# First layer's scores of B with C computed by halves of the source positions, two halves of the array at a time

## The reference, cut to what matters

```python
xc, Bc, Cc = silu(conv(x_ssm)), silu(conv(Bm)), silu(conv(Cm))   # 32 heads: 64, 128, 128 channels
decay = exp(dt * A)
dtx = dt[..., None] * xc
def step(h, inp):
    dec_t, dtx_t, B_t, C_t = inp
    h = dec_t[..., None, None] * h + dtx_t[..., None] * B_t[:, :, None, :]
    return h, einsum('bhpn,bhn->bhp', h, C_t)
y = y * rsqrt(mean(y * y, axis=-1) + 1e-06) * silu(z)
out = y.reshape(B, T, H * P) @ Wout.T
```

## Time and profile before

| what | before |
|---|---|
| time, median of 3 runs | 1088.79 us |
| profiled execution | 1084.22 us, span 1083.0 us, granted clock 0.994 |
| TensorE matmul busy | 1028.9 us (95%) |
| VectorE busy | 798.6 us (74%) |
| ScalarE busy | 614.9 us (57%) |
| GpSimd busy | 696.9 us (64%) |
| scores L778 | 512 instructions, 62.5 us |
| masks L1733 | 64 instructions, 42.3 us |
| first layer | up to about 572 us |

### The profile page before, as it was taken

How to read it: one execution, slowest core, us unless ns; L and a number is a source line. 1 busy time by engine, 2 the same in 40 slices (tenths; PEclk the granted TensorE clock), 3 DMA queues, 4 the chain that set the end, 5 groups by cost and what they waited for, 6 DMA issues and landing times.

```text
span 1083.0 us, 23866 instructions
## 1 busy us (share of the span) xinstructions
PE 1028.9 (95%) x9886; PEld 851.0 (79%) x9886; DVE 798.6 (74%) x1194; ACT 614.9 (57%) x951; POOL 696.9 (64%) x684
## 2 busy tenths in 40 slices
PE   7899999999999999999999899998888889899998
PEld 6688888888888888888887788887554578788887
DVE  5789887888878888788957676455758875686554
ACT  5897877777778778787625222224863553332221
POOL 4977786787867878678782587554266323285553
PEclk9999999999999999999999999999999999999999
DMA  3322211212112121111020553303121120253311
GB/s 111 113 69 79 69 60 50 69 51 69 60 50 69 50 70 59 50 40 51 2 70 4 187 188 103 102 20 108 47 53 23 30 72 2 82 171 108 114 54 40
DMA packets 47453, 76.29 MB, mean 70 GB/s; under 512 B 11430, under 2 KB 34322, under 8 KB 47346
## 3 DMA queue, kind: packets, MB, share of 16 engines
q1 hardware_dynamic: 47346, 74.77, 21.9%
HBM read 68.46 MB, written 2.36 MB: 65 GB/s over the span
## 4 chain that ended last, share of the span: by engine, by line
PE 64%; DVE 19%; POOL 7%; ACT 4%; issue 3%; DMA 1%; SPq 0%; DVEq 0%; POOLq 0%; ACTq 0%
PE psum L698 33%; PE psum L936 8%; DVE arena L1708 6%; PE psum L670 4%; PE psum L786 4%; PE psum L778 3%; PE psum L831 3%; DVE arena L1745 2%; PE psum L1045 2%; PE psum L1009 1%; DVE arena L1982 1%; PE psum L1079 1%; DVE arena L1764 1%; DVE arena L1772 1%; PE psum L1018 1%
## 5 line engine op out<-in xcount | busy, mean ns | idle before, releaser
L698 PE MATMUL psum<-vT,split 128*128 128x512 f32 x2136 | 536.4, 400 | 12.9 <-DVE arena L1708 5.4
L698 PEld LDWEIGHTS psum<-vT,split 128*128 128x128 f32 x2136 | 388.4, 188 | 102.9 <-DVE arena L1708 7.6
L1708 DVE SCALAR_TENSOR_TENSOR arena<-psum,arena 128x1023 f32<-128x1023 f32 (+2 forms) x208 | 265.7, 1278 | 75.5 <-ACT arena L1237 52.3
L2168 POOL TENSOR_TENSOR split<-arena,split 128x256 fp32r<-128x256 f32 x178 | 134.7, 770 | 66.2 <-ACT split L1162 66.0
L2375 POOL TENSOR_TENSOR arena<-arena,bcast 128x512 f32<-128x512 f32 x64 | 85.7, 1341 | 98.8 <-ACT arena L1409 81.8
L1237 ACT ACTIVATE arena<-psum,arena 128x512 f32<-128x512 f32 x160 | 109.3, 691 | 69.9 <-PE psum L698 69.1
L1409 ACT ACTIVATE arena<-psum,arena 128x512 f32<-128x512 f32 x72 | 49.7, 690 | 165.5 <-PE psum L698 164.5
L1860 DVE SCALAR_TENSOR_TENSOR arena<-psum,arena 128x512 f32<-128x512 f32 x72 | 53.9, 749 | 102.7 <-POOL arena L2375 101.0
L936 PEld LDWEIGHTS psum<-split_down,split_hid 128*128 128x128 f32 x864 | 112.6, 191 | 9.5 <-DVE split_hid L1873 3.7
L936 PE MATMUL psum<-split_down,split_hid 128*128 128x256 f32 x864 | 115.2, 283 | 3.0 <-DVE split_hid L1873 3.0
L2195 POOL TENSOR_TENSOR arena<-arena,v 128x1021 f32<-128x1021 f32 x32 | 76.5, 2390 | 42.4 <-DVE arena L1708 42.4
(11 more groups left out here) (228 smaller groups left out, 1519.9 us busy)
## 6 DMA issues: line engine op xcount, KB each, us to landing
bcast<-scratch_a SPq DMA_DIRECT2D x32, 512.0 KB, 3.7
bcast<-scratch_e SPq DMA_DIRECT2D x32, 512.0 KB, 4.2
arena<-in_w_a SPq DMA_DIRECT2D x16, 768.0 KB, 4.4
arena<-in_wg SPq DMA_DIRECT2D x36, 128.0 KB, 3.6
arena<-in_wu SPq DMA_DIRECT2D x36, 128.0 KB, 3.6
arena<-in_wd SPq DMA_DIRECT2D x36, 128.0 KB, 3.9
arena<-in_wout_a SPq DMA_DIRECT2D x8, 256.0 KB, 2.6
arena<-in_w_b SPq DMA_DIRECT2D x10, 128.0 KB, 5.2
```

The lines of the kernel that those rows point to most:

```text
L698: m = pe.matmul(bank, split[:, t % SPLITS, i, q, :], vT[:, j, q, half * BANK:(half + 1) * BANK], start=(n == 0), stop=(n == 3 * KD - 1))
L1708: dve.scalar_tensor_tensor(out=tile[:, s:T], in0=bank[:, 0:T - s], scalar=cw_a[:, j, i, TAPS - 1 - s:TAPS - s], in1=tile[:, s:T], op0=ALU. ...
L2168: pool.tensor_tensor(split[:, t % SPLITS, 1], raw, split[:, t % SPLITS, 0].bitcast(F32), ALU.subtract).then_inc(sem["split"], 1)
```

## The change

For every chunk the scores are computed in two matmuls: `late=0` takes the sources 0 to 63 against all 128 targets, `late=1` the sources 64 to 127 against the targets 64 to 127; the masked quarter isn't computed. For even chunks the first goes to the PSUM partitions 0 to 63 and the second to 64 to 127; for odd chunks it is the other way round. Matmuls of an even and an odd chunk alternate: c late 0, c+1 late 0, c late 1, c+1 late 1. A bank of four chunks has 8 matmuls in place of 4, of 64 output rows each. One semaphore, `masked_a`, is added; nothing waits on it.

The mask, one instruction over 128 partitions and 512 elements before, becomes three: the even chunks of the bank (128 partitions, 256 elements), the odd chunks' sources 0 to 63 (64 partitions, 256 elements, scores read from PSUM partitions 64 to 127), and the odd chunks' sources 64 to 127 (64 partitions, 128 elements, scores read from PSUM partitions 0 to 63). The result lies in SBUF where it lay before.

```diff
+        def half_of(c, late):
+            at = (late + c) % 2 * SUB
+            return slice(at, at + SUB)
...
-                    for i in range(4):
-                        c = 4 * q + i
-                        m = pe.matmul(chunk(bank, i), chunk(cv_a[:, j % 2, 1 + g, :], c),
-                                      chunk(cv_a[:, j % 2, 3 + g, :], c), start=True, stop=True)
+                    def rows(c, late):
+                        ts = slice(late * SUB, P)
+                        return pe.matmul(chunk(bank, c % 4)[half_of(c, late), ts],
+                                         chunk(cv_a[:, j % 2, 1 + g, :], c)[:, late * SUB:(late + 1) * SUB],
+                                         chunk(cv_a[:, j % 2, 3 + g, :], c)[:, ts], start=True, stop=True)
+                    for c in (4 * q, 4 * q + 2):
+                        for late in range(2):
+                            rows(c, late)
+                            m = rows(c + 1, late)
                     m.then_inc(sem["unit"], 1)
...
-                    dve.tensor_tensor(half, bank_of(unit), half, ALU.mult).then_inc(sem["dve_done"], 1)
+                    buf, scores = (ap.rearrange("p (c o t) -> p c o t", o=2, t=P) for ap in (half, bank_of(unit)))
+                    dve.tensor_tensor(buf[:, :, 0], scores[:, :, 0], buf[:, :, 0], ALU.mult).then_inc(sem["masked_a"], 1)
+                    for late in range(2):
+                        own, ts = slice(late * SUB, (late + 1) * SUB), slice(late * SUB, P)
+                        m = dve.tensor_tensor(buf[own, :, 1, ts], scores[half_of(1, late), :, 1, ts], buf[own, :, 1, ts],
+                                              ALU.mult)
+                        m.then_inc(sem["dve_done" if late else "masked_a"], 1)
```

More of the change, by code:

```diff
@@ L338 @@
  tap0 tap term light silu z decay decay_act expo expo_sel expd ud state square sq_sum nrm normed decay_pool nar_zero ln_bias
- bias_hi bias_lo share_hi share_lo gelu gated hid hid_hi hid_lo down down_hi down_lo ones_e router res x_out exp_step
+ masked_a bias_hi bias_lo share_hi share_lo gelu gated hid hid_hi hid_lo down down_hi down_lo ones_e router res x_out exp_step
  bconst cw_half fixed pad piece masked masked_p y_zero gated_hi gated_lo wo_hi wo_lo out_split heads ud_b st_half tile_y y_out squared gates rms x_b x_a x_s out_lo x_lo sq_acc sq""".split()
```

## The result

The changed kernel takes 1122.91 us (median of 4 runs, 1121.12 to 1126.08), the one before 1088.28 (4 runs): ratio 1.0322, 95% interval 1.0296 to 1.0348, or 34.6 us slower. The forecast was 1116.5 us in a range of 1098 to 1124. The profiled execution took 1121.99 us with a span of 1120.8, which is 37.8 more than the span before. The direction and the mechanism are as forecast; of the size 7 us were missing.

A forecast was written before the change was run, and what follows sets the result against it. TensorE and VectorE were taken to bind together; losses of 6.7 (even pairs), 12.6 (odd), 4.7 (1 and 2), 2.25 (0) and 1.4 (15) sum to 27.7 us, giving 1116.5 us on the runs' median, range 1098 to 1124.

The forecast's parts named there:

- What bounds the kernel: First layer: TensorE and VectorE bind at once, a quarter of a microsecond between them; TensorE waits only 7.7 us.
- Cost of a mask: VectorE, L1733: three instructions for one, each starting 0.03 us after the end before; +0.62 us a mask, 64 masks.
- Rival A: VectorE's instructions overlap as now: +0.29 us a mask, 11.0 us in all, 1099.8 us; chance 0.17.
- Array: TensorE's scores, L778: halves run beside each other, 32 instructions in about 1.4 to 1.5 us a stage.
- edges: TensorE, passing between full-array and half-array stages: 0.08 + 0.14 + 0.08 = 0.30 us on the first scores stage, leaving 0.13 saved.
- Rival B: TensorE's scores: halves don't run beside each other in this order; 4.5 us more, 1121 us, stages of 2 us or more; chance 0.07.
- What hides what: Idle on VectorE hides masks: even pairs from 4 +1.12 us, odd from 3 +2.10, pairs 1 and 2 +2.35.
- nearly all for L1764: TensorE's grown idle time in the first layer would be waits for VectorE's last sum of y, some for L2225 and taps.
- some 44 us in the layer: TensorE's idle time in the first layer, grown from 8 us (7.7 + 27.7 + 8.8).
- Rival C: TensorE's saving decides: 8.8 us gained, 1080.0 us; chance 0.06.
- D: Gain and loss cancel within 0.2% (2.2 us), as with a mask cost of +0.1 us; chance 0.04.

The follow-up runs named there:

- filled kernel: Changed kernel plus 6 matmuls of ones ahead of the wait for the normalised y in pairs 1, 2, 4, ..., 14: 1113.47 us, ratio 1.0228.
- masks only: Changed kernel with full 128-column scores, masks still three instructions, odd chunks' scores read from the partitions that are written: 1113.97 us, ratio 1.0242.
- first head only: Against the kernel before: scores and masks by halves for the first head of each pair, second head as before: 1093.03 us, ratio 1.0070.
- whole-banks: Changed kernel with the halves turned over for a whole bank, not every odd chunk; one bank's mask one instruction, the other's two: 1099.94 us, ratio 1.0122.

## Why the prediction was right, and what it missed

- What bounds the kernel: right. With 7.7 us of waits in 480 it looked bound by TensorE, and the two experiments with one half of the change each show that VectorE's chain sets the pace: the array's gain is worth 4.2 us, the masks' loss 26 (the clock's part in it included).
- Cost of a mask, +0.62 us with each start held: right (1.22 measured, 1.22 forecast). Rival A is out; the price of 0.03 behind each instruction is what the traces show.
- Array: 1.48 and 1.39 us a stage, forecast 1.4 to 1.5. The first stage saves 0.22 on 1.70, not 0.13: its edges cost 0.2 together, not 0.30. The second saves 0.49 (324.66 to 326.54 before, 1.88 us). Rival B is out: in the order L R R L the halves run beside each other. The order was right in the prediction, its description not: an odd chunk's second matmul uses the half of the next even chunk's first, not that of its own first.
- What hides what: right in each class of pairs, shown with the clock kept up. The forecast had +1.12 for even, +2.10 for odd pairs, +2.35 for pairs 1 and 2; with the clock kept up they are +1.17, +2.03 and +2.3, and the whole layer +27.8 for 27.7. What TensorE waits for was forecast less well: "nearly all for L1764" is 10.9 of the 34.1 us (L1783 now), GpSimd has 12.9 and the carried states, which the prediction didn't name, 6.9.
- What was missed: the prediction priced TensorE's growing idle time as idle time alone. It named it (some 44 us in the layer; the waits listed came to 34 us from 60 to 540, 39 to 590) and did not ask what an engine does after it. In even pairs the wait for the normalised y went from 0.54 to 1.84 us, and behind it the clock fell. The five falls between 200 and 510 us cost 34.14 - 32.58 = 1.56 us each, 7.8 us, and the sixth, in pair 14, 0.9 (29.51 for 28.60). That is the missing term: 27.7 and 8.7 give 36.4, where the trace has 36.2 in the layer and the medians 34.6. The filled kernel shows it by experiment, not only by the rows. The runs of the changed kernel differ, 1121 to 1126 us at mean clocks of 0.983 to 0.976, so the number of falls probably does too, and the term is less sharp than the others. The profiled execution also has one fall at 27 us, ahead of the first scores, which the kernels with masks only and with the first head only have too and the filled one hasn't. It costs nothing in the end: the first scores of pair 0 begin 1.1 us later than in the filled kernel (53.81, 52.71), those of pair 1 at the same time (85.66, 85.59).
- Rival C, faster, is out. So is D.

## What to carry to other kernels

Before an engine at 95% is relieved, find what it waits for, however little: here 7.7 us of waits in 480 told of a chain that was as long, and whatever is put on that chain counts in full wherever no idle stands behind it. Count the instructions that a layout for one engine asks of another: halves on the array bought 0.2 to 0.5 us a stage and cost three instructions for one, each with its fixed part and a held start. And when a change makes TensorE wait longer, price the clock behind the wait as well, and try filling it.

## What the runs showed of the hardware

- Two neighbours on VectorE overlap by 81 to 85 ns (medians) when they start on the same partitions and stand 31 to 33 ns apart when one starts in the other half: 0.11 us a switch, whether the switch is in the PSUM input (second instruction of the changed mask) or in SBUF (what follows the third).
- fp32 matmuls of 64 output rows, on alternating halves of the columns, run beside each other also in the order L R R L and with 128 and 64 columns of data mixed: 32 instructions in 1.39 to 1.48 us. In all 64 banks the instruction that carries the bank's semaphore, the last one issued, starts 6 to 7 ns before another one of the same bank, so the recorded starts aren't in program order. The Trainium skill has a rule of strict program order for starts and ends ("TensorE: Matmul & The Clock Gate", "The mechanism"). By that rule an estimate, rival B's nine slots of 0.056 us for two chunks, is 2.0 us a stage; the measurement decides.
- A wait of 1.84 us on TensorE, with one of 0.44 soon after it, was followed by the lower clock (a projection of 4.25 us for 3.05); with 1.5 us of it filled and 0.50 left it wasn't. The length of the wait alone doesn't tell: of the 24 waits of 1.54 to 1.88 us for the normalised y in the traces of the changed, the masks-only and the whole-banks kernel, 12 have a fall behind them. In pairs 1 and 2 of the changed kernel the clock held behind 1.88 and 1.84 us, with whole banks it fell there behind 1.84 and 1.83 and held behind six of 1.68 to 1.69. What decides between them isn't shown.
